# A graph layer on one core: projection to expert as one program, selections formed one place ahead, edge batches dealt anew

## What is computed

```python
xn = layernorm(x)
# 1: graph part
agg = segment_sum(edge_attr, dst) / max(count, 1)
g = xn + relu(concat([xn, agg]) @ W1 + b1) @ W2 + b2       # 576 -> 1024 -> 512
# 2: attention part, 8 heads, with sums over all tokens in i, o, i_hat, o_hat
q, k, v = split(xn @ W_qkv.T + b_qkv); q = sigmoid(q); k = sigmoid(k)
i = sum(q * sum(k, tokens)); o = sum(k * sum(q, tokens))
i_hat = sum(q * sum(k / o, tokens)); o_hat = sum(k * sum(q / i, tokens))
kv = einsum('bshd,bshe->bsde', k, v * softmax(o_hat, tokens))
a = (einsum('bshd,bsde->bshe', q / i, kv) * sigmoid(i_hat)) @ W_out.T + b_out
x = x + g + a
# 3: one expert of 16, chosen by the mean of all normalised tokens
xn = layernorm(x); scores = softmax(mean(xn, tokens) @ Wg + bg); e = argmax(scores)
x = x + scores[e] * (xn @ We[e] + be[e])
```

## Time and profile before

| | us |
|---|---|
| median of 3 runs (2226.78 to 2238.92) | 2229.93 |
| the profiled execution, its time | 2234.79 |
| its span in the trace | 2233.1 |
| PE busy | 1920.9 (86%) |
| PEld busy | 1522.4 (68%) |
| DVE busy | 1222.2 (55%) |
| ACT busy | 560.4 (25%) |
| POOL busy | 1341.5 (60%) |
| mean granted clock of PE | 0.903 |

### The profile page before, as it was taken

The page is one execution under the profiler, slowest core; times in us unless marked ns, Lnnn a source line. Parts: engine busy times, 40 slices in busy tenths (PEclk is TensorE's granted clock), DMA queues, the critical chain, the costliest instruction groups (busy, mean ns, idle before and its releaser), DMA issues. The chain is left out here.

```text
span 2233.1 us, 31150 instructions
## 1 busy us (share of the span) xinstructions
PE 1920.9 (86%) x10775; PEld 1522.4 (68%) x10775; DVE 1222.2 (55%) x3855; ACT 560.4 (25%) x1314; POOL 1341.5 (60%) x876
## 2 busy tenths in 40 slices
PE   2899999999999999688758877777855999998698
PEld 1688887788888788344347766666644888886586
DVE  3534435434344432477565655565536888884575
ACT  2322233322232222111122112111212333332210
POOL 3688888888888888777688878878850000000100
PEclk9899999999999999666867789898777999999799
DMA  9878777787787777887999999999856766652784
GB/s 270 191 154 152 142 139 150 149 153 151 133 160 141 136 142 125 230 206 166 268 228 176 183 189 163 182 202 160 151 98 197 228 207 209 200 180 97 264 303 146
DMA packets 516664, 397.45 MB, mean 178 GB/s; under 512 B 348027, under 2 KB 385163, under 8 KB 516510
## 3 DMA queue, kind: packets, MB, share of 16 engines
q1 hardware_dynamic: 387758, 340.83, 54.5%
q0 software_dynamic: 126640, 54.59, 24.0%
q10 hardware_dynamic: 2112, 0.07, 0.1%
HBM read 242.42 MB, written 152.96 MB: 177 GB/s over the span
## 5 line engine op out<-in xcount | busy, mean ns | idle before, releaser
L286 POOL DMA_INDIRECT table<-edge_sums,edge_row x831 | 1310.8, 1577 | 341.0 <-issue 253.7
L230 DVE SCALAR_TENSOR_TENSOR edge_sel<-edge_dst_all,edge_dst_f,upper 128x128 f32<-128x128 int16 x831 | 316.9, 437 | 105.0 <-PE edge_sum L242 104.8
L338 PE MATMUL pr_out_bank<-pr_norm_xT_hi,pr_w_hi 128*128 128x512 f32 (+1 forms) x832 | 330.1, 397 | 0.0
L338 PE MATMUL pr_out_bank<-pr_norm_xT_lo,pr_w_hi 128*128 128x512 f32 (+1 forms) x832 | 321.1, 386 | 0.0
L338 PE MATMUL pr_out_bank<-pr_norm_xT_hi,pr_w_lo 128*128 128x512 f32 (+1 forms) x832 | 320.9, 386 | 0.0
L242 PEld LDWEIGHTS edge_sum<-edge_attr,edge_sel 128*128 128x128 f32 x1662 | 230.6, 210 | 131.8 <-DVE edge_sel L230 106.5
L242 PE MATMUL edge_sum<-edge_attr,edge_sel 128*128 128x65 f32 x1662 | 244.9, 296 | 80.0 <-DVE edge_sel L230 79.7
L252 ACT ACTIVATE edge_sums<-edge_sum 128x260 f32<-128x260 f32 (+1 forms) x209 | 80.5, 386 | 578.0 <-PE edge_sum L242 546.1
L338 PEld LDWEIGHTS pr_out_bank<-pr_norm_xT_lo,pr_w_hi 128*128 128x128 f32 x832 | 156.8, 188 | 33.8
L338 PEld LDWEIGHTS pr_out_bank<-pr_norm_xT_hi,pr_w_lo 128*128 128x128 f32 x832 | 157.3, 189 | 29.5
L338 PEld LDWEIGHTS pr_out_bank<-pr_norm_xT_hi,pr_w_hi 128*128 128x128 f32 x832 | 157.2, 189 | 28.9
(11 more groups left out here) (202 smaller groups left out, 3254.2 us busy)
## 6 DMA issues: line engine op xcount, KB each, us to landing
edge_dst_all<-dst SPq DMA_DIRECT2D x103, 256.0 KB
edge_attr<-in_edge_attr SPq DMA_DIRECT2D x103, 256.0 KB
qk_T<-pr_stage SPq DMA_DIRECT2D x48, 512.0 KB, 3.3
h_pre_T<-pr_stage SPq DMA_DIRECT2D x48, 512.0 KB, 3.4
gn_pre<-h_pre_T SPq DMA_DIRECT2D x12, 2048.0 KB, 9.6
done<-qk_T SPq DMA_DIRECT2D x16, 1024.0 KB, 6.7
table<-edge_sums,edge_row POOLq DMA_INDIRECT x831
pr_norm_x<-in_x SPq DMA_DIRECT2D x12, 1024.0 KB, 8.6
```

What stands on the lines that cost most here:

```text
L230: op = dve.scalar_tensor_tensor(out=self.sel[q][0:rows, j, 0:rows], in0=self.dst_all[k][0:rows, t:t + m * (rows - 1) + 1:m], scalar=self.d ...
L286: pool.indirect_dma_start(self.c.table[t], bass.IndirectOffsetOnAxis(ap=self.row[k][0:rows, j:j + 1], axis=0), self.sums[k][0:rows, j, :], ...
L338: mm = pe.matmul(out, a, c, start=first and i == 0, stop=last and i == n - 1)
```

## The change

- Front, gnn and expert become one program with a queue of work per engine; each stage's function now returns the engines' parts. The constants stay a program of their own. What the barriers ordered is now ordered by semaphores: gnn's table loads wait for `front_done`, which POOL raises after it has waited for the last stores of `base` (`over`), cleared the same 74 semaphores and seen the last scatters land. All other semaphores of attend, gnn and expert live to the end.
- gnn's weights are loaded by attend's SP program in its tail block (`preload`), before the tail's store of `base`, and split ahead of `front_done` (the two pieces of W2 partly after it). The buffers' order in SBUF changes so that this is possible.
- Block 0 of gnn: PE multiplies hidden piece j by W2 as soon as j is ready, and forms piece j + 3 ahead of it. `hid` has four buffers.
- x1 is kept in four buffers of one subtile and stored by subtile; POOL waits for the store two before.
- The expert's mean is formed after the last token sum; SP loads xT of block 0 early; each piece of weights and the bias row have a semaphore of their own, and PE takes the pieces of block 0's first subtile as they come. The output's stores have a semaphore for each of two buffers, and the stage's loops are written out.
- In project, DVE forms at place g the selection of place g + 1 (at the last place that of the next block's first).
- SHARE_B has 12 batches instead of 9, SHARE_D 31 instead of 34.

The diff, cut to its core:

```diff
-SHARE_B = [1, 1, 1, 0, 1, 1, 1, 0, 1, 1, 1, 0, 0]
+SHARE_B = [1, 1, 1, 1, 1, 1, 1, 1, 1, 1, 1, 1, 0]
 SHARE_C = [1, 0, 0, 1, 0, 0, 1, 0, 0, 1, 0, 0, 0]
-SHARE_D = [3, 3, 3, 3, 3, 3, 3, 3, 3, 3, 3, 1, 0]
+SHARE_D = [3, 3, 3, 3, 3, 3, 3, 3, 3, 2, 2, 0, 0]
...
+    def next_quads(b, k, g, places):
+        if g + 1 < places:
+            return quad_at(b, k).get(g + 1, [])
+        return quad_at(b + 1, 1 - k).get(0, []) if b + 1 < NB else []
...
             for g, (kind, i) in enumerate(groups(n)):
-                for quad in quads.get(g, []):
+                if b == 0 and g == 0:
+                    for quad in quads.get(0, []):
+                        edges.select(dve, *quad)
+                for quad in next_quads(b, k, g, len(groups(n))):
                     edges.select(dve, *quad)
...
+            if b == NB - 1:
+                me.preload(sp)
             sp.wait_ge(acc_free, b * CH + len(subtiles(n)))
...
+    def over(eng):
+        eng.wait_ge(acc_free, FULL * CH + 1)
+        for k in range(2):
+            eng.wait_ge(stored[k], 16 * len(range(k, NB, 2)))
...
+    def preload(sp):
+        sp.wait_ge(before.mixed, FULL * before.STEPS)
+        weights.load(sp)
...
+        sp.wait_ge(c.front_done, 1)
+        load_tables(0, BT)
-            weights.load(sp)
...
-            weights.wait(pe)
-            for j in range(JH):
-                hidden(0, 0, BT, j)
-            output(0, 0, BT, 0)
+        weights.wait(pe, 2)
+        for j in range(BANKS):
+            hidden(0, 0, BT, j)
+        for j in range(JH):
+            if j + BANKS < JH:
+                hidden(0, 0, BT, j + BANKS)
+            if j == 0:
+                weights.wait(pe, 4)
+                pe.wait_ge(x1_ready, 1)
+            pe.wait_ge(h_ready, j + 1 + HIDS)
+            mm = products(pe, acc[0][:, :], [(h_hi[0][:, j, 0:P], h_lo[0][:, j, 0:P])],
+                          [(w2_hi[:, j, :], w2_lo[:, j, :])], first=j == 0, last=j == JH - 1)
+        mm.then_inc(acc_mm, 1)
...
+        dve.wait_ge(before.mixed, FULL * before.STEPS)
+        weights.split_lo(dve, 0, 2)
+        dve.wait_ge(c.front_done, 1)
+        add_tables(0, BT)
+        divide_sums(0, BT)
+        weights.split_lo(dve, 2, 3)
+        split_agg(0, 0, BT)
+        dve.wait_ge(b1_in, 16)
+        add_pre(0, 0, BT, 0)
+        add_pre(0, 0, BT, 1)
+        weights.split_lo(dve, 3, 4)
+        for j in range(JH):
+            low(0, 0, BT, j)
+            if j + 2 < JH:
+                add_pre(0, 0, BT, j + 2)
...
+        def store_x1(b, n, s):
+            r = subtiles(n)[s]
+            pool.wait_ge(x1_ready, b * CH + (AHEAD + s + 1))
+            if b or s >= 2:
+                pool.wait_ge(x1_stored[s % 2], b * 32 + s // 2 * 16)
+            pool.dma_start(c.x1[bass.ds(b * BT + s * P, r), :], x1[s][0:r, :]).then_inc(x1_stored[s % 2], 16)
...
+        sp.wait_ge(before.x1nT_stored[0], 16)
+        sp.wait_ge(before.hid_ready, before.AHEAD + FULL * JH)
+        sp.wait_ge(before.x1_ready, before.AHEAD + FULL * CH)
+        load_xT(0, 0, BT)
+        sp.wait_ge(gate_step, 13)
+        for k in range(2):
+            sp.wait_ge(before.x1_stored[k], FULL * 32 + 16 * (1 - k))
+            sp.wait_ge(before.x1nT_stored[k], 16 * len(range(k, NB, 2)))
+        for ch in range(CH):
+            sp.wait_ge(gathered[ch], 16)
+        load_x1(0, 0, BT)
...
+        for ch in range(CH):
+            act.wait_ge(gathered[ch], 16)
+            act.activation(w_hi[:, ch, :], w_raw[:, ch, :], ACT.Copy).then_inc(w_hi_ready, 1)
...
+        dve.wait_ge(before.parts_added, FULL * CH + 2)
+        step(dve.tensor_scalar(mean[:, :], c.token_sum[:, :], 1.0 / TOKENS, None, ALU.mult))
...
+            edges.scatter_all(pool)
+            attend.over(pool)
+            for sem in project.sems + norms.sems + scale.sems + edges.sems:
+                pool.sem_clear(sem)
+            edges.finish_pool(pool)
+            pool.sem_inc(c.front_done, 1)
```

945 lines of the change are left out of this document (464 added, 481 removed).

## The result

The kernel after takes 2216.69 us, median of 7 runs (2203.80 to 2218.99), beside 2233.11 for the kernel before: a ratio of 0.9916, 95% interval 0.989 to 0.9943. The forecast was 2197, with a range of 2180 to 2214. The sign was right; the gain is half of what was forecast (16.4 us of 32.9), and the median lies 2.7 us above the range.

The account below looks back on a forecast made before the run. PE bounds the front, POOL's scatters a second bound beside it; PE sets gnn's pace. Terms -2 - 2 - 15.5 - 13.8 = -33.3 took 2234.8 to 2201.5; as that run lay 4.9 above the median, 2197, range 2180 to 2214.

Parts of the forecast that it names:

- early selections: Projection: selections one place ahead let PE gain only some 6 us, worth 6.1 us of POOL's idle.
- lead limit: Projection and attend: PE leads POOL by at most 19 tiles, 35 us; in attend it binds from about the sixth block.
- POOL's idle: Norms and scale: four POOL stops, 28.8 us, are filled; POOL ends 28 us earlier, near 1629.
- Attend: Attend: ninth block's store at 1547, 105.6 us more to the last store near 1652.5, -2 us.
- price of 2.4 us a quad: Attend after the ninth block: each of six quads less saves 2.4 us, 14.4 together; bounds some 1 to 3.2.
- Rival C: Attend ends later: more landing waits, or quads save only 1 us; last store +14 to +20, 2216; chance 0.1.
- First border: Last store of `base` to first table load: store 3.5, clears 6, 10 us instead of 12.2; -2 us (+1 to -8).
- rival B: A border gives little: dearer clears, loads stuck behind preloaded weights, or late fourth gather; 12 us lost, 2209; chance 0.17.
- Weights preloaded, first block interleaved: gnn's start: first table load to second block's hidden layer takes 33.3 us instead of 48.8, -15.5 us.
- x1's quarter stores: gnn: four x1 stores for one add 36 POOL issues of some 0.75 us, under 26.8 us of cover; nothing.
- rival D: gnn slower: x1 stores landing above 13.4 us cost 24 per microsecond; 2235 at about 15 us; chance 0.04.
- Second border: gnn to expert: earlier mean, -8.5, and weights freed from the bias row, with a new wait of some 2.3; -13.8 us.

Follow-up runs that it names:

- sel_back: Kernel after with the projection's selections formed at their own place again, the new dealing kept; ratio 0.9911 to the kernel before.
- clears_early: Kernel after with POOL's semaphore clears moved ahead of its wait for the last stores of `base`; ratio 0.9909 to the kernel before.
- Group 2: Kernel after unchanged (ratio 0.9918 to the kernel before), and with one batch moved from the projection to attend in three variants (0.9846, 0.9910, 0.9843).
- share_56: Kernel after with one batch moved from the projection's twelfth block to attend's tenth; ratio 0.9846 to the kernel before.
- both_back: Kernel after with the projection's old order of selections and the old dealing of batches; ratio 0.9889 to the kernel before.
- Group 4: Runs with 32 bytes of unused SBUF buffer: two on the kernel after (ratios 0.9931, 0.9891 to the kernel before), one on share_56 (0.9833).
- w2_shift: Kernel after with 32 bytes of unused buffer around W2's pieces, so that only W2 moves in SBUF; ratio 0.9931 to the kernel before.
- gn_shift: Kernel after with 32 bytes of unused buffer ahead of W2's low part, moving W2 and the hidden layer's buffers; ratio 0.9891 to the kernel before.

## Why the prediction was half right

**The step that failed** is that of the early selections and what follows for attend's start: "By the lead limit PE may gain only some 6 us there", and "PE comes only some 5 us later (12 less 6)". I had seen the limit and took it for a cap on a gain. But the engine that reaches it stops, and a stop can cost more than the limit caps. PE gained 23 us in eleven blocks (the waits had shown 12.3), lost 8.5 to POOL in the twelfth, and 21 in the tail, 18 of them by the clock. Attend started 11.1 us later (1145.21 against 1134.08), not 5. The new dealing alone makes that 9.6 us (sel_back, 1143.65), about the 10 to 12 that were forecast for norms; it is the 6 us of the selections that failed: they gave 1.6 us of loss instead. Nor were 6 us the cap: with the clock kept (clears_early) attend starts 17 us sooner than without the early selections. Group 2 shows the cause by taking one batch away.

**POOL's idle.** "POOL's idle of 28.8 us is filled" held for three of the four stops. The first isn't one of dealing: POOL drains the last batch of the projection and waits for norms, and norms came later. It grew from 6.1 to 10.0 us beyond the usual step, so of the 28.8 us only some 18 were saved: POOL's last scatter came 18.4 us sooner instead of 28. That also refutes the claim that batch 58 "can follow batch 57 at once"; it does so in share_56 and clears_early, where PE is through early and at full clock, and whose traces have no stop there.

**Attend.** Ninth store at 1557.3 (forecast 1547), because POOL was late by those 10 us and by smaller waits; from there to the last store 111.0 us (forecast 105.6), so six quads less, with a wait of 10.0 us still in it (2 were assumed), gave 12.3 us where 17.8 were expected. The price of 2.4 us a quad is not borne out either: between both_back and sel_back six quads less shorten attend by 2.0 us in all, because POOL holds those blocks, and the new dealing alone makes the median 4.4 us longer (2208.68 beside 2204.29, ranges that overlap). Rival C described this end (+14 to +20; it was +14.0). Its quads that save little are part of what happened; the stop in the projection was in no rival. Its time, 2216, is what came out; it had a chance of 0.1.

**First border.** Sum of 10 us, measured 15.55: clears 5.8 (assumed 6), store 9 (assumed 3.5). The two sides of the bound were stated as +1 to -8; +3.3 is outside. Of the 5.7 us that the store took beyond its 3.5, 3 are the weights ahead of it in the queue, as rival B had it, and the rest is the store itself.

**Weights preloaded, first block interleaved.** 31.99 us, forecast 33.3. This step, the largest, was right, and so were the nothing for x1's quarter stores (they land in 4.6 us, more than the 2.6 estimated in rival D and far from its 13.4) and the mean: it is formed 0.2 us behind the last token sum.

```profile
2054.04 0.16 DVE L1975 TENSOR_TENSOR token_sum<-token_sum,gn_part 128x4 f32<-128x4 f32 x1 [1.43 <-ACT gn_x1nT L1869]
2054.24 0.17 DVE L2224 TENSOR_SCALAR ex_mean<-token_sum 128x4 f32<-128x4 f32 x1
```

**Second border.** -13.8 forecast, -10.1 measured. PE's first product came 21 us sooner (2065.47 against 2086.48) and its wait before block 1 was 2.55 us (forecast 2.3). But the load of xT for the second block stands behind the fourth gather, and ACT could split that piece only at 2069.73, 11.5 us behind the row numbers; in the kernel before SP went on 11.6 us behind them, with the bias row as the fifth. "The fourth about 1.8 us before the bias row" was not borne out: in the kernel after the fourth piece comes as late behind the row numbers as the bias row did before, so dropping the wait for the bias row gave nothing there.

```profile
2069.73 0.63 ACT L2203 ACTIVATE ex_w_hi<-ex_w_raw 128x512 fp32r<-128x512 f32 x1 [2.12 <-DMA ex_w_raw<-in_w_exp,ex_row]
2077.83 1.92 ACT L2195 ACTIVATE ex_xT_hi<-ex_xT 128x2048 fp32r<-128x2048 f32 x1 [7.47 <-DMA ex_xT<-x1n_T]
```

**gnn's pace.** Nothing forecast, -5.0 measured, by the operands' places in SBUF (Group 4). The account: 16.0 us of miss in the front (6 of them at attend's start, 10 in attend), 5.3 at the first border and 3.7 at the second, 25.0 together; gnn and the end of the span took 6.1 off again and the first block 1.3, which leaves the 17.5 us between forecast and trace.

**The rule weighed ahead.** The port pair of DVE and GpSimd (the Trainium skill, SBUF — State Buffer, section SBUF: two separate sides) could have stretched the scatters beside more selections, if a scatter counts as a read of SBUF. From 960 to 1000, with a batch beside every norms block, 22 scatters take 33.60 us, 1.53 each, beside DVE 77% busy; no run here shows that lock.

## What to carry to other kernels

Where two engines are coupled by a bounded lead, work out when a faster one will reach the bound, not only how much it may gain: from there on each microsecond saved is a stop, and a stop can cost the clock of what follows, as it did in this tail. An edit that speeds up one side is then worth nothing until work is dealt anew to match; here moving one batch of 105 was enough (share_56). Look for the stop of the engine that bounds the stage, not for the wait of the engine behind it: here ACT waited 7.88 us and PE only 2.96, and where ACT waited 4.64 PE didn't stop at all. When loads are pulled ahead, ask what small store on the critical path they will stand in front of, and what housekeeping stands behind it.

## What the runs showed of the hardware that was not expected

In gnn a product of 128x512 of the same work started every 0.2333 us (kernel before; 0.2326 in w2_shift) when its two operands start at different remainders modulo 64 bytes in SBUF, and every 0.2279 or 0.2274 us (kernel after, gn_shift) when the remainders are equal. In the projection the remainders are equal and the interval is 0.233, so equal remainders are not enough everywhere.

74 semaphore clears on POOL took 5.8 us, 0.08 each (clears_early beside the kernel after).

Behind a stop of PE of 1.64 to 4.84 us, a tail of 106-column products stayed at the lower clock for some 37 us with PE busy, in each of the seven traces that have such a stop. The same instructions without that stop kept the full clock (clears_early). That is 16 to 20 us in the projection's end: 886.0 against 902.3 to 905.9.
